# A fused attention and gated-FFN layer on eight cores: the q transposes and the LayerNorm sums issued later in each tile, k's norm written to a buffer of its own

## What is computed

```python
xn = (x - mean(x)) / sqrt(var(x) + 1e-5)
q, k = l2norm(heads(xn @ Wq.T)), l2norm(heads(xn @ Wk.T))
v = heads(xn @ Wv.T)
attn = softmax(q @ k.T + where(0 <= rel < 128, -abs(rel) * slope[h], -1e30))
s = concat(attn @ v) @ Wo.T
h = silu(xn @ (wg/127).T) * (xn @ (wu/127).T)
g = silu(h @ (wd/127).T)
out = x + s * g
```

## Time and profile before

| | us |
|---|---|
| median of 3 runs (lowest, highest) | 4348.65 (4344.25, 4388.81) |
| the profiled execution's own time | 4342.89 |
| its span on the slowest core (7) | 4341.3 |
| spans of the 8 cores | 4323.3 to 4341.3 |
| mean granted TensorE clock of each core | 0.92 to 0.93 of full speed |

### The profile page before, as it was taken

The page is one execution under the profiler, slowest core; times in us unless marked ns, Lnnn a source line. Parts: engine busy times, 40 slices in busy tenths (PEclk is TensorE's granted clock), DMA queues, the critical chain, the costliest instruction groups (busy, mean ns, idle before and its releaser), DMA issues.

```text
span 4341.3 us, 59912 instructions; the slowest of 8 cores (4323.3 to 4341.3 us)
## 1 busy us (share of the span) xinstructions
PE 3476.6 (80%) x20160; PEld 1660.6 (38%) x20160; DVE 1223.2 (28%) x2246; ACT 1956.2 (45%) x2875; POOL 131.3 (3%) x292
## 2 busy tenths in 40 slices
PE   2523578888888898888888798888888898889887
PEld 1212333443434343443434343443434343444443
DVE  0101122314233232324233232324233233324141
ACT  4324421635545362635445363635445362635352
POOL 1001000000000000000000000000000000000000
PEclk6666689999999999999999999999999999999999
DMA  6666634434343435434443434434343435334342
GB/s 143 149 154 146 127 121 148 139 119 163 122 152 129 149 117 159 137 125 157 123 145 123 159 117 159 137 129 154 123 148 127 150 120 166 128 117 165 105 151 92
DMA packets 276420, 596.39 MB, mean 137 GB/s; under 512 B 71072, under 2 KB 71072, under 8 KB 258720
## 3 DMA queue, kind: packets, MB, share of 16 engines
q1 hardware_dynamic: 236192, 464.63, 33.4%
q0 software_dynamic: 39936, 127.94, 10.9%
HBM read 558.92 MB, written 60.82 MB: 143 GB/s over the span
## 4 chain that ended last, share of the span: by engine, by line
PE 55%; DMA 14%; ACT 12%; issue 9%; DVE 9%; POOL 0%; SPq 0%; DVEq 0%; ACTq 0%; POOLq 0%
PE psB L520 11%; PE psB L537 11%; PE psA L497 8%; PE psA L563 7%; PE psB L563 6%; PE psA L689 5%; DMA WA<-wdT_s 4%; PE psA L609 3%; DVE STAT L455 3%; DVE GBUF L582 2%; ACT GBUF L578 2%; ACT GBUF L384 2%; ACT GBUF L380 2%; ACT AOF L680 1%; DMA WGU<-wgT_s 1%
## 5 line engine op out<-in xcount | busy, mean ns | idle before, releaser
L497 PE MATMUL psA<-WA,XN 128*128 128x512 bf16 x3072 | 754.2, 407 | 296.1 <-DVE TM L465 153.8
L537 PE MATMUL psB<-XN,WGU 128*128 128x512 bf16 x3072 | 736.9, 383 | 39.4 <-ACT GBUF L578 29.7
L520 PE MATMUL psB<-XN,WGU 128*128 128x512 bf16 x3072 | 731.7, 381 | 18.9 <-DMA WGU<-wgT_s 15.1
L497 PEld LDWEIGHTS psA<-WA,XN 128*128 128x128 bf16 x3072 | 312.8, 103 | 730.8 <-issue 427.5
L545 DVE TENSOR_TENSOR HID<-psB,TSC 128x512 bf16<-128x512 f32 x384 | 262.6, 691 | 809.9 <-PE psB L537 447.6
L537 PEld LDWEIGHTS psB<-XN,WGU 128*128 128x128 bf16 x3072 | 300.8, 98 | 415.4 <-issue 65.3
L520 PEld LDWEIGHTS psB<-XN,WGU 128*128 128x128 bf16 x3072 | 284.6, 98 | 354.3 <-issue 36.7
L578 ACT ACTIVATE GBUF<-psA,CST 128x1024 f32<-128x1024 f32 x32 | 35.7, 1115 | 808.5 <-PE psB L563 763.1
L627 DVE TENSOR_TENSOR PT<-PT,EB 128x512 bf16<-128x512 bf16 x496 | 211.1, 426 | 595.6 <-ACT PT L622 572.4
L528 ACT ACTIVATE TSC<-psB,CST 128x512 bf16<-128x512 f32 x384 | 259.7, 687 | 257.2 <-PE psB L520 255.1
L689 PE MATMUL psA<-WA,AOF 128*128 128x512 bf16 x1024 | 240.8, 389 | 110.3 <-ACT AOF L680 91.5
(11 more groups left out here) (88 smaller groups left out, 2805.7 us busy)
## 6 DMA issues: line engine op xcount, KB each, us to landing
WGU<-wgT_s SPq DMA_DIRECT2D x384, 256.0 KB, 2.7
WGU<-wuT_s SPq DMA_DIRECT2D x384, 256.0 KB, 2.7
WD<-wdT_s SPq DMA_DIRECT2D x96, 512.0 KB, 4.8
WA<-wdT_s SPq DMA_DIRECT2D x96, 512.0 KB, 3.9
XL<-x POOLq DMA_DIRECT2D x16, 2048.0 KB, 12.0
WA<-wkT_s SPq DMA_DIRECT2D x32, 1024.0 KB, 7.8
WA<-wvT_s SPq DMA_DIRECT2D x32, 1024.0 KB, 7.6
XE<-x POOLq DMA_DIRECT2D x16, 2048.0 KB, 9.2
```

What stands on the lines that cost most here:

```text
L497: last = e.matmul(psA[:, 512 * tc:512 * tc + 512], XN[p1][:, 512 * dc + 128 * tc:512 * dc + 128 * tc + 128], wap[:, 512 * dc:512 * dc + 51 ...
L520: last = e.matmul(psB[:, go:go + 512], gap[:, goff + 128 * dc:goff + 128 * dc + 128], XN[p][:, 512 * dc:512 * dc + 512], start=(dc == 0), ...
L537: last = e.matmul(psB[:, uo:uo + 512], uap[:, uoff + 128 * dc:uoff + 128 * dc + 128], XN[p][:, 512 * dc:512 * dc + 512], start=(dc == 0), ...
```

## The change

It moves four things, and gives k's norm another target.

1. `norm_apply` writes k's result to PT instead of TM (`_nbuf` chooses), and `kq_transpose` reads it there. PT is the buffer of the attention's exponentials, which is idle at this point. The two slots that the prologue's weight loads have in PT (`pinw_pool`) are recorded against the same buffers.
2. q's transposes go behind both halves of the k projection, and so does `ln_stats(g + 2)`.
3. k's transposes go behind both halves of the v projection.
4. The filler calls are spread differently: 1+1 behind the q halves (1+2 before), 1+1 behind the k halves (1+2 before), 1 behind q's transposes (as before), 1+1 behind the v halves (as before), 2 behind k's transposes (1 before). That is 9 units ahead of the attention where there were 10; the one left over is done behind the attention, where `tile` empties the list. In tile 15, which has no k and v, it is 8 instead of 10.

```diff
+        def _nbuf(which, tc, eh):
+            if which == "q":
+                return TM, bTM4[tc]
+            col = 1024 * tc + 512 * eh
+            return PT, bPT[col // 2048][(col % 2048) // 512]
...
-            (PT[:, 2048 * i:2048 * i + 1536], bPT2[i]) for i in range(2)]
+            (PT[:, 2048 * i:2048 * i + 1536], [bPT2[i]] + bPT[i][0:3])
+            for i in range(2)]
...
-                filler(1 + eh)
-            kq_transpose(g, QF, bQF, "qT", range(TCN))
-            filler(1)
-            has_ln = g + 2 < n_iters
-            if has_ln:
-                ln_stats(g + 2)
-
+                filler(1)
             if g + 1 < n_iters:
                 wk_s = load_wa("wk", 0, f"wk0_{g}"), load_wa("wk", 1, f"wk1_{g}")
                 for eh in range(2):
                     for tc in proj_eh(g + 1, eh, wk_s[eh], pn, "kproj"):
                         norm_apply(g + 1, "k", eh, tc)
-                    filler(1 + eh)
-                kq_transpose(g + 1, KF[pn], bKF[pn], "kT", range(TCN))
+                    filler(1)
+                kq_transpose(g, QF, bQF, "qT", range(TCN), which="q")
                 filler(1)
+                if has_ln:
+                    ln_stats(g + 2)
                 wv_s = load_wa("wv", 0, f"wv0_{g}"), load_wa("wv", 1, f"wv1_{g}")
...
                     filler(1)
+                kq_transpose(g + 1, KF[pn], bKF[pn], "kT", range(TCN), which="k")
+                filler(2)
             else:
+                kq_transpose(g, QF, bQF, "qT", range(TCN), which="q")
+                if has_ln:
+                    ln_stats(g + 2)
                 filler(6)
```

More of the change, by code:

```diff
@@ L276, in _prep_in @@
             ap, bf = pool[s]
+            bfs = bf if isinstance(bf, list) else [bf]
             P.op(q, (lambda e, sem, ap=ap, nm=nm, rows0=rows0, ncols=ncols,
@@ L282, in _prep_in @@
                                  ).then_inc(sem, 16)),
-                 writes=[bf], tag=f"pin_{nm}_{rows0}_{cols0}")
-            return ap, bf
+                 writes=bfs, tag=f"pin_{nm}_{rows0}_{cols0}")
+            return ap, bfs[0]
         def _prep_T(inap, inbf, nblk, bank, tag, ps=None, bps=None):
@@ L451, in norm_apply @@
             bS = bSQ2[tc % 2]
+            dst, bdst = _nbuf(which, tc, eh)
             P.op("act", (lambda e, tc=tc, sqo=sqo: e.activation(
@@ L464, in norm_apply @@
                  reads=[bN], writes=[bN])
-            P.op("dve", (lambda e, eh=eh, tc=tc, N8=N8: e.tensor_tensor(
-                TM[:, 1024 * tc + 512 * eh:1024 * tc + 512 * eh + 512].rearrange(
+            P.op("dve", (lambda e, eh=eh, tc=tc, N8=N8, dst=dst: e.tensor_tensor(
+                dst[:, 1024 * tc + 512 * eh:1024 * tc + 512 * eh + 512].rearrange(
                     "p (h c) -> p h c", h=8),
@@ L469, in norm_apply, with kq_transpose, tfn @@
                 st(N8, 8).unsqueeze(2).broadcast_to([128, 8, 64]), ALU.mult)),
-                reads=[bpsA[tc], bN], writes=[bTM4[tc]], tag=f"{which}nrm{g1}_{eh}_{tc}")
-        def kq_transpose(g1, DST, bDST, tag, tcs):
+                reads=[bpsA[tc], bN], writes=[bdst], tag=f"{which}nrm{g1}_{eh}_{tc}")
+        def kq_transpose(g1, DST, bDST, tag, tcs, which="q"):
             for tc in tcs:
-                def tfn(e, tc=tc):
+                srcs = [_nbuf(which, tc, eh) for eh in range(2)]
+                sap = srcs[0][0]
+                sbufs = [b for (_a, b) in srcs]
+                def tfn(e, tc=tc, sap=sap):
                     last = None
@@ L721, in tile @@
             load_xe(g, f"ldxe{g}")
+            has_ln = g + 2 < n_iters
             for eh in range(2):
@@ L852, in build_nc @@
                 norm_apply(0, "k", eh, tc)
-        kq_transpose(0, KF[0], bKF[0], "kT", range(TCN))
+        kq_transpose(0, KF[0], bKF[0], "kT", range(TCN), which="k")
         wv_s = load_wa("wv", 0, "wv0_p"), load_wa("wv", 1, "wv1_p")
```

4 lines of the change are left out of this document (2 added, 2 removed).

## The result

| | before | after |
|---|---|---|
| median of the runs, us (lowest) | 4350.05 (4341.01) | 4401.94 (4382.21) |
| ratio of fast runs | | 1.0089, 95% interval 1.0065 to 1.0114 |
| profiled execution, us | 4342.89 | 4389.15 |
| spans of the 8 cores, us | 4323.3 to 4341.3 | 4357.0 to 4387.6 |

Both programs also have executions in which one die's cores run at a lower clock; the ratio leaves them out, the two medians do not. The change costs 0.9%, some 39 us (0.0089 x 4350): above the range on record, which ended at 4386, and well above its 4351.

The account below looks back on a forecast made before the run. ACT's order of norms and LayerNorm sums was taken to set the tile's pace, so PE's wait would only move. Terms +10 + 6.5 + 3.5 - 18 = +2 on the profiled 4342.9, plus 5.8 to the median: 4351 us, range 4318 to 4386.

Parts of the forecast that it names:

- the wait moves, not goes: Tiles 1 to 13: PE's wait for the sums moves from k's second half to v's; 4351 us, chance 0.52.
- c: Tiles 1 to 13: PE's clock loss behind the wait for v, between 0 and 2.5 us, taken as 1.2.
- +10 for the 13 tiles: Tiles 1 to 13: +0.8 us per tile (-0.4 to +2.1), together +10 us (-5 to +27).
- PE leaves q's transposes at the lower level: Tiles 1 to 13: PE's clock is low after q's transposes; wait for v 2.5 us rather than 5, sum the same.
- The tenth unit follows behind the attention, 3.45: Tiles 1 to 13: the FFN unit moved behind the attention costs 3.45 us, its SiLU covered.
- SP passes wk's loads two units earlier and wo's one unit later: Tiles 1 to 13, SP: shifted weight loads cost nothing, with 13.8 us or more before each first use.
- PE waiting for a load: Sign that wo came late through an SP wait; tiles 1 to 13 had no such wait in this stretch before.
- tile 0, -18 (-35 to +7): Tile 0: wk, wv and wo are issued earlier, wo by 21 us; 3 us come back through a seventh chunk.
- two slow and two fast: Tile 0: pricing the four chunks' stores ahead of wo's loads this way puts wo at 453, before 473.99.
- Tile 14: +6.5 (5 to 8): Tile 14, without sums: 69.6 us from q's end, against 64.2 before, and up to 2.5 of clock.
- Tile 15: +3.5 (3 to 5): Tile 15, without k: 37.3 us and the clock, against 34.3 before.
- Rival (c): Slower: clock drops in every wait for v, four slow chunks eat tile 0's gain; +47 us, 4396, chance 0.2.

Follow-up runs that it names:

- e1: Changed kernel with the load of wq's second half (`nwq1`) recorded behind the last FFN units instead of ahead of them; ratio to the kernel before 0.9998.
- e9: Changed kernel with a unit's FFN weights recorded three units ahead instead of two, `nwq1` left in place; ratio to the kernel before 1.0040.
- e2: Kernel before with only the FFN unit behind v's second half taken out and done behind the attention; a single execution, 4388.7 us.
- e6: Changed kernel with a third unit behind k's transposes, so ten units stand ahead of the attention again; ratio to the kernel before 1.0052.
- e11: Changed kernel with, in tile 0 only, wq's and wo's loads recorded right behind v's second half, ahead of the chunks' stores; ratio to the kernel before 1.0119.
- e7: Changed kernel with ten units ahead of the attention and the LayerNorm sums moved into the down projection; ratio to the kernel before 0.9970.

## Why the prediction was wrong

**Where it held.** It followed ACT through the tile and forecast that the wait moves, not goes: the norm waits fall, transposes wait longer (73.8 us in all, 41.0 before), v's second half waits once a tile, 79.1 us behind q (79.3). A and its unit: 102.43 against a forecast of 102.47 - 0.4 + c, so c comes to 0.4. The 104 halves of v say the same: 26 of them lost 1.7 us, the rest nothing. The forecast had taken 1.2, half of its only row, and that is the 10 us by which its +10 for the 13 tiles misses the measured -0.5, inside its -5 to +27. It also held that PE leaves q's transposes at the lower level: their last two took 1.01 each. The Trainium skill (TensorE: Matmul & The Clock Gate, part 4) has it that transposes do not count for the clock. The earlier trace rows and these transposes do not show that, for PE also waited 1.3 to 1.7 us between them; and another place speaks against it. Kernel before, core 7, tile 0:

```profile
331.15 2.11 PE L295 MATMUL psB<-IDT,HID 128*128 128x128 bf16 x16 [5.93 <-ACT WGU L330]
333.35 1.01 PE L295 MATMUL psB<-IDT,WD 128*128 128x128 bf16 x8
334.16 2.34 PE L478 MATMUL psA<-IDT,TM 128*128 128x128 bf16 x32
336.33 0.61 PE L295 MATMUL psB<-IDT,WD 128*128 128x128 bf16 x8
```

PE does nothing but transposes here, and in the midst of them the granted clock rises from 0.50 (331.2 to 334.9) to 0.99 (334.9 to 337.9): eight take 1.01 us first and 0.61 later. So transposes alone did bring the clock back. The forecast's sum did not hang on the rule.

**The step that failed first: "The tenth unit follows behind the attention, 3.45", and with it "SP passes wk's loads two units earlier and wo's one unit later" at nothing.** Of the queues that the moved unit is moved past, the forecast followed PE's and ACT's, and on SP only wk's and wo's loads. (In recorded order wo's loads come one unit earlier, not later; no tile behind tile 0 waits for them.) It never looked at `nwq1`, a load that waits for the end of the attention and that, with the tenth unit moved, stands ahead of unit 23's loads. In place of 3.45 per tile: 4.05 in the mean of ten tiles, 7.62 in three, and 0.54 in each stretch D: 27 us beyond the unit. The forecast sentence also named what would show it, "PE waiting for a load", but looked for that only ahead of the attention. e1 and e9, two unlike edits, remove most of it; e2 brings it into the old order; e6 takes the unit back and it is gone.

**The second: tile 0, -18 (-35 to +7), was 0.** The first two thirds of the chain are exact (wk, k's norms, wv, v within 3 us). The error is the price of the four chunks of stores: 24.86, 8.04, 11.89 and 13.39 us [after], 58 in all, where I took "two slow and two fast", 44.

The reason given, "since before, too, just the first two were slow", misread the kernel before: its fast pair (6.84 and 6.83, from 406.81 on) ran while GpSimd issued no cast load at all for 43.26 us, held up by PE, which was itself waiting for wv. And the two chunks right ahead of wo took 12.46 and 20.47. In the changed kernel wv comes sooner, PE and the casts go on, and GpSimd issues 9, 3, 2 and 4 cast loads beside the four chunks; the DMA engines are busy 97, 59, 71 and 81% (52% beside the fast pair). wo came at 465.6, inside 436 to 478; that says little, as the bounds were 42 us wide.

The remaining lead was given back in the attention: from scores to the first output projection 51.6 us (37.5 before), and from there to the first gate matmul 84.6 (80.2), means over the cores. The Trainium skill (DMA: Bandwidth & Descriptors, SWDGE vs HWDGE vs iDMA) says that an engine takes turns between the two kinds of queue; the forecast set it aside for two fast chunks in the trace of before, and by it no gain was to be expected. That is what came, and the trace agrees in the main: from wv's load on, each chunk with cast loads beside it took longer than 6.85, from 8.04 to 24.86. What e11 adds is that an earlier wo would not have helped.

**Tile 14: +6.5 (5 to 8) was +7.8. Tile 15: +3.5 (3 to 5) was +5.9**: above its bounds. In tile 15 (core 5) the fourth transpose ends 10.3 us behind the end of q (forecast 9.7), the clock costs 1.4 behind it (the forecast named it and gave it only 0.5), and q's second half is 0.4 longer. Two units behind the attention cost 6.96, as priced.

**Sum by terms.** Forecast +10 + 6.5 + 3.5 - 18 = +2. Measured -0.5 + 7.8 + 5.9 + 0, +27 behind the attention, -3 at the start, +0.5 at the end: +38, against the stretches' +37. Two missed terms of 27 and 18 us, softened by 10 us too much in the steady tiles. Rival (c), slower, came nearest in size (+47 against +39), in part by luck: its clock loss in each tile did not come (0.4 us and not 2.5); its half on tile 0, four slow chunks that eat the gain, was right.

**What stays open.** That cast loads slow the stores is read from the traces; no run took them away. Nor is it known why `nwq1` hurt only 13 of the 80 ordinary stretches, or which loads make the 0.54 in D. e9 and e1 leave B 0.05 above the unit's 92.76 + 3.45 and J at 94.4 (91.28 + 3.45 is 94.7), so in B and J nothing is left to explain.

## What to carry to other kernels

When a change moves a piece of work, follow every queue that the piece feeds, the weight loads' above all, to the first instruction there that waits: one load that waits for a late event, recorded ahead of an urgent one, cost more here (27 us) than all that the change did to the engine it aimed at. Before moving what waits, ask which engine sets the pace of the stretch: moving the transposes and the sums within it gave nothing, taking the sums out of it gave 3%. And compare a reordering with the bottleneck removed too, for the engine that sets the pace can hide what the new order costs (8.3 us per tile in e7, nothing in e6). Before the price of a fast case is used, look at what else ran beside it: the two fast chunks of before had the DMA engines half free.
